# Split operands for the adapter's two products in a four-stage residual kernel on one core

## The reference, cut to what matters

```
Wd, bd = down_w[profile_ids], down_b[profile_ids][:, None]     # 512 x 128
Wu, bu = up_w[profile_ids], up_b[profile_ids][:, None]         # 128 x 512
z = relu(einsum('bsh,bhk->bsk', hidden, Wd) + bd)
y = hidden + einsum('bsk,bkh->bsh', z, Wu) + bu
mu, var = mean(y), mean(square(y - mu))
x3 = hidden + (y - mu) * rsqrt(var + EPS) * g + b              # hidden is x2, the stencil's result
```

## Time and profile before

| | |
|---|---|
| median of 3 runs | 709.85 us (706.27 to 1123.24) |
| profiled execution | 705.1 us |
| its span in the profile | 703.3 us |
| PE, DVE, ACT, POOL busy | 95%, 75%, 52%, 26% of the span |
| mean granted clock of TensorE | 0.986 of 2.4 GHz |

### The profile page before, as it was taken

The page is one execution under the profiler, slowest core; times in us unless marked ns, Lnnn a source line. Parts: engine busy times, 40 slices in busy tenths (PEclk is TensorE's granted clock), DMA queues, the critical chain, the costliest instruction groups (busy, mean ns, idle before and its releaser), DMA issues.

```text
span 703.3 us, 8054 instructions
## 1 busy us (share of the span) xinstructions
PE 665.5 (95%) x2792; PEld 487.1 (69%) x2792; DVE 529.5 (75%) x744; ACT 363.8 (52%) x745; POOL 185.5 (26%) x262
## 2 busy tenths in 40 slices
PE   4969997999699999999999999999999999999996
PEld 1534444478477868786878687868786878687875
DVE  2676788939996888688868886888689649864965
ACT  1143376665366356636653665456535653565145
POOL 5003430305344205420542144114511210111001
PEclk9999999999899999999999999999999999999999
DMA  7996999999404660466147514751465230022001
GB/s 206 318 336 227 256 185 297 302 258 311 86 3 98 144 116 11 95 142 113 16 90 153 101 23 100 142 97 25 125 99 98 33 87 1 0 43 79 0 1 60
DMA packets 51670, 85.77 MB, mean 122 GB/s; under 512 B 8480, under 2 KB 10528, under 8 KB 51630
## 3 DMA queue, kind: packets, MB, share of 16 engines
q0 software_dynamic: 16896, 33.56, 29.3%
q1 hardware_dynamic: 31230, 51.69, 21.2%
q10 hardware_dynamic: 3504, 0.01, 0.3%
HBM read 63.22 MB, written 22.04 MB: 121 GB/s over the span
## 4 chain that ended last, share of the span: by engine, by line
PE 82%; DVE 7%; DMA 5%; ACT 4%; SPq 1%; issue 1%; POOLq 0%; POOL 0%; ACTq 0%; DVEq 0%
PE bank L1133 21%; PE bank L1134 21%; PE bank L1135 21%; PE bank L1188 4%; PE bank L1178 3%; PE bank L1034 3%; PE bank L1129 3%; DVE tr L1664 2%; DMA beside_scratch<-xb 2%; PE bank L1168 2%; PE bank L1197 2%; DMA xr<-beside_scratch 2%; DMA xts<-in_xT 1%; PE bank L1228 1%; DVE wgb L1651 1%; PE bank L1130 1%
## 5 line engine op out<-in xcount | busy, mean ns | idle before, releaser
L1664 DVE TENSOR_TENSOR_SCAN tr<-alpha,carry,tr 128x512 f32<-128x512 f32 x48 | 58.8, 1267 | 0.0
L845 ACT ACTIVATE carry<-tr 128x2 f32<-128x2 f32 x32 | 6.6, 205 | 89.4 <-DVE tr L1664 89.4
L1133 PE MATMUL bank<-th,wg_l 128*128 128x512 f32 x128 | 52.0, 406 | 0.0
L1133 PE MATMUL bank<-xh,wg_l 128*128 128x512 f32 x128 | 52.0, 406 | 0.0
L1134 PE MATMUL bank<-tl,wg_h 128*128 128x512 f32 x128 | 50.5, 395 | 0.0
L1134 PE MATMUL bank<-xl,wg_h 128*128 128x512 f32 x128 | 50.5, 395 | 0.0
L1135 PE MATMUL bank<-xh,wg_h 128*128 128x512 f32 x128 | 50.2, 392 | 0.0
L1135 PE MATMUL bank<-th,wg_h 128*128 128x512 f32 x128 | 50.2, 392 | 0.0
L1651 DVE SCALAR_TENSOR_TENSOR wgb<-wgb,soma 128x512 f32<-128x512 f32 x32 | 25.9, 811 | 25.0 <-ACT wgb L839 25.0
L626 POOL TENSOR_TENSOR rs_a<-ss_a,consts 128x1 f32<-128x1 f32 x32 | 14.3, 447 | 113.2 <-ACT junk L795 112.7
L863 ACT ACTIVATE wide<-bank,bias_temp 128x512 f32<-128x512 f32 x32 | 21.9, 683 | 31.3 <-PE bank L1135 31.3
(11 more groups left out here) (264 smaller groups left out, 1984.8 us busy)
## 6 DMA issues: line engine op xcount, KB each, us to landing
x2b<-beside_scratch POOLq DMA_DIRECT2D x12, 1024.0 KB, 9.3
xr<-rows_scratch POOLq DMA_DIRECT2D x10, 1024.0 KB, 10.3
xb<-in_x SPq DMA_DIRECT2D x8, 1024.0 KB, 14.3
result<-xr SPq DMA_DIRECT2D x7, 1024.0 KB, 4.2
x2b<-rows_scratch POOLq DMA_DIRECT2D x6, 1024.0 KB, 9.5
x_scratch<-xb SPq DMA_DIRECT2D x5, 1024.0 KB, 8.0
beside_scratch<-xts SPq DMA_DIRECT2D x5, 1024.0 KB, 10.7
late_y<-x_scratch SPq DMA_DIRECT2D x20, 256.0 KB, 2.7
```

What stands on the lines that cost most here:

```text
L1133: pe.matmul(acc, wl, xh_, start=start, stop=False)
L1664: ve.tensor_tensor_scan(t[:, d], alpha[:, 1 + d:2 + d].broadcast_to([P, GN]), t[:, d], 0.0 if first else carry[:, k, 1 + d:2 + d], ALU.mul ...
```

## The change

From block 1 on the adapter's two products are made by `split3`. ScalarE writes x2 transposed straight into the high part (`x2h`, same memory as `wide`); VectorE's new `x2_lo` makes the four low parts from PSUM into four buffers that are free at that time (`junk`, `junk_o`, `late_y`, `late_side`). `relu` is evaluated twice, once as fp32 and once as high part `z_h`, and VectorE's new `z_low` subtracts. `down` waits for each `x2_lo`, `up` for `z_low`. The weights are split once per batch, by `adapter_hi` on ScalarE and `adapter_lo` on VectorE, in groups 0 and 3, and there is one set of them: batch 1's adapter is loaded at the start of group 3, after `up(3)`. Block 0 keeps its fp32 products (`first_down`, `first_up`). The first late tile of a block is loaded only after `down` of the block two before it, and its POOL work waits for that block's `up`, since their buffers now hold low parts.

```diff
@@ -81,8 +81,10 @@
         wn1_st, wn1_l = staged("wn1_l", [P, KE, A])
 
-        dw = sb("dw", [P, B, KE, A])
-        uw = sb("uw", [P, B, E])
+        dw_room, dw_h = staged("dw_h", [P, KE, A])
+        dw_st, dw_l = staged("dw_l", [P, KE, A])
+        uw_room, uw_h = staged("uw_h", [P, E])
+        uw_st, uw_l = staged("uw_l", [P, E])
         xr = sb("xr", [P, 2, GT, E])
@@ -97,8 +99,8 @@
         ln_g_row = sb("ln_g_row", [P, B, E])
         gamma_row = sb("gamma_row", [P, E])
-        nar = sb("nar", [P, GN])
-        junk_sb = sb("junk", [P, GN])
+        nar, nar_r = staged("nar", [P, GN])
+        junk_sb, junk_r = staged("junk", [P, GN])
 
@@ -109,8 +111,8 @@
         def load_adapter(sp, b, pid):
             one = bass.ds(pid, 1)
-            sp.dma_start(dw[:, b], down_w[one].rearrange("o (k p) a -> p (o k) a", p=P)).then_inc(lw_in[b], 16)
-            sp.dma_start(uw[:, b], up_w[one].rearrange("o a e -> (o a) e")).then_inc(lw_in[b], 16)
+            sp.dma_start(dw_st[:], down_w[one].rearrange("o (k p) a -> p (o k) a", p=P)).then_inc(lw_in[b], 16)
+            sp.dma_start(uw_st[:], up_w[one].rearrange("o a e -> (o a) e")).then_inc(lw_in[b], 16)
 
@@ -129,7 +131,7 @@
 
             x2b0 = sb2("x2b0", [P, GT, E])
-            wide = sb2("wide", [P, KE, GN])
+            wide, wide_r = staged("wide", [P, KE, GN], s2)
             tr = sb2("tr", [P, 2, 2, GN])
@@ -145,9 +147,9 @@
             xh_room = sb2("xh", [P, KE, PAD + GN], F32R)
             xl_room = sb2("xl", [P, KE, PAD + GN], F32R)
-            late_y = sb2("late_y", [P, E])
-            late_side = sb2("late_side", [P, E])
-            junk_o = sb2("junk_o", [P, E])
+            late_y, late_y_r = staged("late_y", [P, E], s2)
+            late_side, late_side_r = staged("late_side", [P, E], s2)
+            junk_o, junk_o_r = staged("junk_o", [P, E], s2)
 
@@ -165,6 +167,9 @@
             return rooms[g % 2][i][:, :, PAD + GN - 1]
 
+        x2h, x2l = wide_r[:], [t[:] for t in (junk_r, junk_o_r, late_y_r, late_side_r)]
+        z_h, z_l = late_side_r[:], nar_r[:]
+
         def x3_pair(g):
...
@@ -425,6 +434,8 @@
                             sp.wait_ge(late_chan, 3 * n)
                         sp.wait_ge(x1_out[q], 16)
+                        if c == 0:
+                            sp.wait_ge(down_mm, q - 1)
                         sp.dma_start(late_y[:], x1_rows(q)[:, c]).then_inc(late_in, 16)
@@ -494,13 +505,13 @@
                     sp.wait_ge(x1_out[7], 16)
                     sp.dma_start(wt_st[:], chunks(wtemp)).then_inc(w2_in[1], 16)
-                    sp.wait_ge(blog_set, B)
-                    sp.wait_ge(score_use, B * NG)
-                    load_adapter(sp, 1, sp.value_load(ids[0:1, 1:2], min_val=0, max_val=7))
 
                     out_v = out.rearrange("b (u c p) e -> p (b u) c e", p=P, c=GT)
 
                     for g in range(GROUPS - 1):
+                        if g == NG - 1:
+                            sp.wait_ge(up_mm, GT * NG)
+                            load_adapter(sp, 1, sp.value_load(ids[0:1, 1:2], min_val=0, max_val=7))
                         if g + 3 < GROUPS:
@@ -579,6 +590,8 @@
                         if late_tile(q, c):
                             po.wait_ge(late_done, late_tile(q, c))
+                        if c == 0:
+                            po.wait_ge(up_mm, GT * (q - 1))
                         po.tensor_tensor(late_side[:, 1:E - 1], late_y[:, 0:E - 2], late_y[:, 2:E], ALU.add)\
@@ -778,13 +791,24 @@
                         for k in ks:
                             act.wait_ge(x2T_mm, KE * q + k + 1)
-                            act.activation(wide[:, k], bank[X2T(q)[k]][:], ACT.Identity,
+                            act.activation(x2h[:, k] if q else wide[:, k], bank[X2T(q)[k]][:], ACT.Identity,
                                            bias=up_cols[:, q // NG, k:k + 1]).then_inc(x2T_ev, 1)
 
                     def relu(q):
                         act.wait_ge(down_mm, q + 1)
                         act.activation(z[:], bank[DOWN(q)][:], ACT.Relu, bias=db_cols[:, q // NG:q // NG + 1])\
                            .then_inc(z_act, 1)
+                        if q:
+                            act.activation(z_h, bank[DOWN(q)][:], ACT.Relu, bias=db_cols[:, q // NG:q // NG + 1])\
+                               .then_inc(z_act, 1)
+
+                    def adapter_hi(b):
+                        act.wait_ge(lw_in[b], 32)
+                        if b == 0:
+                            act.wait_ge(blog_set, B)
+                            act.wait_ge(score_use, B * NG)
+                        act.activation(dw_h[:], dw_st[:], ACT.Copy).then_inc(aw_hi, 1)
+                        act.activation(uw_h[:], uw_st[:], ACT.Copy).then_inc(aw_hi, 1)
 
@@ -979,6 +1003,8 @@
                         keep_ctx(g, 2)
                         sigmoid_gate(g, 2)
+                        if g == 0 or g == NG - 1:
+                            adapter_hi((g + 1) // NG)
                         trace_hi(g, 1)
@@ -1169,23 +1195,35 @@
 
                     def down(q):
-                        b = q // NG
-                        pe.wait_ge(lw_in[b], 32)
-                        pe.wait_ge(x2T_ev, KE * q + 3)
+                        pe.wait_ge(aw_lo, 2 * (q // NG + 1))
+                        for k in ks:
+                            pe.wait_ge(x2T_lo, KE * (q - 1) + k + 1)
+                            last = split3(bank[DOWN(q)][:], dw_h[:, k], dw_l[:, k], x2h[:, k], x2l[k],
+                                          k == 0, k == KE - 1)
+                        last.then_inc(down_mm, 1)
+
+                    def up(q):
+                        pe.wait_ge(z_lo, q)
+                        for c in range(GT):
+                            split3(bank[UP(q)[c]][:], z_h[:, chunk(c)], z_l[:, chunk(c)], uw_h[:], uw_l[:],
+                                   True, True).then_inc(up_mm, 1)
+
+                    def first_down():
+                        pe.wait_ge(lw_in[0], 32)
+                        pe.wait_ge(x2T_ev, 3)
                         for k in ks:
                             if k == KE - 1:
-                                pe.wait_ge(x2T_ev, KE * q + KE)
-                            last = pe.matmul(bank[DOWN(q)][:], dw[:, b, k], wide[:, k], start=(k == 0),
+                                pe.wait_ge(x2T_ev, KE)
+                            last = pe.matmul(bank[DOWN(0)][:], dw_st[:, k], wide[:, k], start=(k == 0),
                                              stop=(k == KE - 1))
                         last.then_inc(down_mm, 1)
 
-                    def up(q):
-                        b, g = q // NG, q - 1
-                        pe.wait_ge(z_act, q + 1)
+                    def first_up():
+                        pe.wait_ge(z_act, 1)
                         for c in range(GT):
-                            if q == 0 and c >= 2:
+                            if c >= 2:
                                 pe.wait_ge(y_add, c - 1)
-                            pe.matmul(bank[UP(q)[c]][:], z[:, chunk(c)], uw[:, b], start=True, stop=True)\
+                            pe.matmul(bank[UP(0)[c]][:], z[:, chunk(c)], uw_st[:], start=True, stop=True)\
                               .then_inc(up_mm, 1)
@@ -1362,10 +1400,10 @@
                     pooled(1, 2)
                     pooled(1, 3)
-                    down(0)
+                    first_down()
                     pooled(1, 4)
                     pooled(1, 5)
-                    up(0)
+                    first_up()
                     for c in range(6, NT):
@@ -1606,6 +1644,23 @@
                         ve.scalar_tensor_tensor(x2_of(q)[:, c], late_side[:], coef[:, ZX, b:b + 1], x2_of(q)[:, c],
                                                 ALU.mult, ALU.add).then_inc(late_done, 1)
+
+                    def adapter_lo(b):
+                        ve.wait_ge(aw_hi, 2 * (b + 1))
+                        if b == 0:
+                            ve.wait_ge(up_mm, GT)
+                        ve.tensor_tensor(dw_l[:], dw_st[:], f32(dw_h[:]), ALU.subtract).then_inc(aw_lo, 1)
+                        ve.tensor_tensor(uw_l[:], uw_st[:], f32(uw_h[:]), ALU.subtract).then_inc(aw_lo, 1)
+
+                    def x2_lo(q):
+                        for k in ks:
+                            ve.wait_ge(x2T_ev, KE * q + k + 1)
+                            ve.scalar_tensor_tensor(x2l[k], bank[X2T(q)[k]][:], up_cols[:, q // NG, k:k + 1],
+                                                    f32(x2h[:, k]), ALU.add, ALU.subtract).then_inc(x2T_lo, 1)
+
+                    def z_low(q):
+                        ve.wait_ge(z_act, 2 * q + 1)
+                        ve.tensor_tensor(z_l, z[:], f32(z_h), ALU.subtract).then_inc(z_lo, 1)
 
@@ -1796,9 +1851,15 @@
                         trace_lo(g, 1)
                         logits(g, 3)
+                        if g == 0 or g == NG - 1:
+                            adapter_lo((g + 1) // NG)
```

(13 more changed lines are left out.)

## The result

| | before | after |
|---|---|---|
| median of the runs, us | 708.73 (4 runs, lowest 706.27) | 718.34 (4 runs, 715.05 to 720.95) |
| profiled execution, us | 705.1 | 718.73 |
| its span, us | 703.3 | 716.8 |
| mean granted clock | 0.986 | 0.981 |

The changed kernel is slower by the ratio **1.0146 (95% interval 1.0097 to 1.0196)**. One run of the kernel before, 1123.24 us, was far slower than the other three and is left out of the ratio, but not of the median in the table.

A forecast was written before the change was run, and what follows sets the result against it. The prediction took TensorE as the bound, busy 665.5 of 703.3 us. It summed 705.1 us (profiled run) + 4.3 (groups 1 to 6) + 4.5 (group 0) = 713.9, say 714, range 705 to 722.

The forecast's parts named there:

- The direction and the mechanism: Groups 1 to 5: slower, since up waits for VectorE's new work and TensorE's saving in down becomes a pause.
- The terms of VectorE's work: VectorE: 0.66 us per x2_lo operation, everything behind 2.2 us later; z_low starts after 0.58 and takes 0.67.
- the +3.5 of the forecast: up can start 3.5 us after trace_lo(g,2)'s old start: 2.2 + 0.58 + 0.67 + 0.05 for the hand-over.
- so I take this stretch as rigid: From the temporal product's end to the next group's logits: 24.6 us of late-tile work, unchanged in groups 1 to 5.
- The second term: Groups 1 to 6: ends move by +0.9, +0.9, +2.2, +0.3, +0.8, -0.8 us, in sum +4.3.
- Group 0: down(1) waits for x2_lo behind logits(0,3), then runs at 1.2 GHz; up ends 4.5 us later, bounds +4.2 to +7.
- Rival 1: Groups 1 to 6: TensorE's saving arrives, 2 x 0.65 us each, giving 701.8 us; chance 0.08.
- Rival 2: Groups 1 to 5: the pause ahead of up drops the clock, +2.5 us a group, giving 726 us; chance 0.12.
- The clock in group 3 alone: Group 3: only its 3.5 us pause ahead of up drops the clock, +2.5 us, giving 716 us; chance 0.18.
- Put at nothing: Second relu, adapter_hi, first late tile's later load, POOL's wait for up, adapter 1's load, later y work: no cost.

The follow-up runs named there:

- e3: The changed kernel without x2_lo and z_low, the third product reading the high part again; 0.9983 of the time of the kernel before.
- e5: The changed kernel with POOL's 1 MB transfer add_shift issued later, behind the transfers of block g+3; 1.0036 of the kernel before.
- e1: The changed kernel with only up split: down stays plain fp32 and x2_lo is gone; 1.0003 of the kernel before.
- e9: e5 with four places in the orders changed (adapter 0's split, x2_lo(1), adapter 1's load and split, z_low ahead of trace_lo(g,2)), all work kept; 0.9932 of the kernel before.
- e7: The changed kernel with add_shift moved and x2_lo ahead of logits(g,3), z_low ahead of traces(g,3)'s scans, relu ahead of gelus, adapter split earlier; 0.9972 of the kernel before.
- e6: The kernel before with only the add_shift transfer moved, the same edit as in e5; 1.0013 of the kernel before.
- e12: e9 with the three subtracts that split the mixer's weights in group 0 made on VectorE instead of POOL; 0.9882 of the kernel before.
- e11: The changed kernel with z_low ahead of trace_lo(g,2) and nothing else; 1.0137 of the kernel before, span 713.5 us.
- e2: The changed kernel with only down split: up stays fp32, z_low and the second relu are gone; 1.0090 of the kernel before.
- e13: e12 with the second of the three subtracts moved ahead of x2_lo(1); 0.9876 of the kernel before, median 697.09 us.

## Why the prediction was right, and where it was not

**The direction and the mechanism were right.** TensorE's saving became a pause, most of it ahead of `up`, because VectorE, only 1.3 us ahead there, got some 3.5 us of new work in front of it. e3 shows it from the other side: without that work the whole 1.26 us a group arrive. What the forecast had at nothing is that `down` itself would wait for the first `x2_lo` in groups 1 to 4 (0.46, 1.24, 2.63 and 0.40 us). It cost nothing more: group 5, without such a wait, is off its forecast by the same 0.3 us as these.

**The terms of VectorE's work were right.** 0.66 us for each `x2_lo`, 0.58 for `z_low`, 0.58 for each `adapter_lo`; `up(2)` at 268.05 is 8.52 us behind the old start of `trace_lo(1,2)`, of which 5.0 had been lost before group 1's `logits`, which leaves the +3.5 of the forecast. From `logits` to `trace_lo(g,2)` the changed kernel takes 2.17 us longer (2.2 forecast). The split product runs at 0.232 us as in the earlier trace rows. By the formula of the Trainium skill (TensorE: Matmul & The Clock Gate, section Back-to-back issue gap) it would be 0.216 (the section gives it for an isolated product), and the measurement decides.

**The mis-sized term is the step "so I take this stretch as rigid", 24.6 us from the temporal product to `logits(g+1,0)`: +2.5 us in all, of the 4.7 that were missing.** It was read from one group; the others of that trace have 24.7 to 24.9 us too, so what was missing was to ask what it is made of. By groups 0 to 4 it grew by 0.1, 0.9, 1.5, 0.5 and -0.6 us. The largest piece is in group 2, where the load of tile 1 took 9.2 us to land. In groups 1 and 3 that load was as before, and the last load of the stretch took 3.6 and 3.3 us in place of 2.7; e3 has the same, and why is open. e5 shows what holds the stretch together: the load shares the DMA engines with a transfer of 1 MB whose reader, `out_apply`, starts over 80 us after it. Without it the stretch is 21.4 in every group, and 10 of the 13.5 us of span are gone. Why the transfer is slower in group 2 (11.8 us in the changed kernel and in e1, against 9.8 to 10.2 in groups 0, 1 and 3; 10.5 before) is open: the slices show a moment of near standstill in its middle that the other groups do not have.

**The second term is 0.3 us a group, 1.8 in all.** 0.16 of it is a reading error: the chain's row for `up` begins at 261.48, TensorE's timeline of the kernel before has its first matmul at 261.32. 0.10 is the first product behind a pause, which is 0.33 us ahead of the next in place of 0.23. The last 0.4 us are in the column of group 0.

**Group 0** was forecast at +4.5 and measured at +5.5; it shows as +4.9 because the first stage happened to be 0.6 us shorter, which is luck. The pause (12.3 us), the low clock in `down` (188.86 to 194.1) and the order of releases are as worked out. Of the 1.0 us, 0.35 is `down`'s later start, 0.4 are the first two products of `soma_in(0,3)`, which still ran at 1.2 GHz, and 0.2 is the chain's reading again.

**Rival 1** (the saving arrives) is false for this kernel, but not for the change: e9 is that case, once VectorE's lateness is gone. **Rival 2** (the clock falls in each pause) is false: behind the pauses of 0.4 to 1.65 us of groups 1, 2, 4, 5 and 6 the granted clock stays at 1.00. It was nearer than its two rows made it look: the trace of before has the low clock also behind three pauses of 1.25 us with a few short transposes between them (the granted clock, 0.50, stands behind POOL's column):

```profile
48.20:51.60 3.40, 3.40 (x8) 2.18 (x9) 0.18 (x1) 0.60 (x1) 0.00 (x0) 0.50 1.03 383
```

**The clock in group 3 alone** did fall, but not ahead of `up` behind a pause of 3.5 us, as the rival had it: it fell in `down(4)`, behind 2.63 us. It cost nothing in place of 2.5 us: it made `down(4)` 1.5 us longer, and `up(4)` still had to wait for `z_low`, which ends at 413.36. **Put at nothing** and found so: the second relu, `adapter_hi`, POOL's wait for `up`; the first late tile's mix stands 2.25 us behind the transposes before and after.

## What to carry to other kernels

When the bounding engine's work is made cheaper by giving preparatory work to another engine, the price is read first at one place: how early that engine is where the new wait will stand. If it is less than the new work, the saving turns into a wait, and in these runs an order that fills the other engine's idle holes got it back (e9 beside e5: all work kept, 1.0036 to 0.9932), while another order of the same work did not (e7, 0.9972). A stretch that looks rigid should be asked what it is made of, even where it is equally long in every group: here a load took 7.6 us where others of its size took 2.6, because it competed with a transfer that could run elsewhere. Moving it was worth nothing while TensorE decided (e6) and 8 to 10 us as soon as VectorE did (e5). And where a trace is one execution, a difference at one place is counted from a point near it, since the first stage alone moved by up to 5 us between executions.

## What the runs showed of the hardware

- A subtract of 128x2048 between SBUF tiles on POOL (4.5 to 5.1 us) stops VectorE for most of its length: a pair of scans takes 7.2 us in place of 2.3, a multiplication 4.5 in place of 0.7. On VectorE the same subtract takes 2.28 us (e12). The Trainium skill (SBUF — State Buffer, section Who interferes with whom) tells of an exclusive lock on a port pair that the two engines share, taken where VectorE's instruction has two inputs in SBUF and GpSimd's reads SBUF. Both stopped operations have two inputs in SBUF, and the traces agree.
- TensorE's clock does not go by the length of a pause alone in these traces. Behind pauses of 0.4 to 1.65 us (the changed kernel, groups 1, 2, 4, 5 and 6) and of 2.45 us (e11, `down(4)`) it stayed at 2.4 GHz. Behind 1.79 us (e2, `down(4)`) and 2.63 us (the changed kernel, `down(4)`) eight products ran at 1.2 GHz, from the third on. Behind 2.88 us it was low for six products (e13), behind 4.6 us for twelve (e12), behind 12.3 us for fourteen (the changed kernel), and behind 13.1 us for seven (e5).
- A load of 256 KB lands in some 2.7 us alone and in 6.4 to 9.7 us beside POOL's `add_shift` of 1 MB, which itself takes 9.8 to 12.2 us there (11.8 and 9.2 in group 2 of the changed kernel).
